# Reordered loads, conversions and squares in the opening of a gated cross-attention and FFN block

## The reference

```python
q1 = fake_quant(layernorm(x), s1, z1)            # clip(round(v / s + z), 0, 255), minus z, times s
q2 = fake_quant(ctx, s2, z2)
x  = x + tanh(g_xattn) * (q1 @ q2)
weight = U * S[None, :] @ V.T                     # U (2048, 512), V (2048, 512)
x  = x + tanh(g_ffn) * einsum('bti,oi->bto', layernorm(x), weight)
```

## Time and profile before

| what | value |
|---|---|
| median of 3 runs | 604.24 us |
| the profiled execution's own time | 604.71 us |
| its span | 602.9 us |
| TensorE matmuls busy | 582.7 us, 97% |
| VectorE busy | 381.7 us, 63% |
| ScalarE busy | 212.4 us, 35% |
| GpSimd busy | 191.4 us, 32% |
| DMA engines, opening (10 to 60 us) | 387 to 393 GB/s without a pause |

### The profile page before, as it was taken

The page is one execution under the profiler, slowest core; times in us unless marked ns, Lnnn a source line. Parts: engine busy times, 40 slices in busy tenths (PEclk is TensorE's granted clock), DMA queues, the critical chain, the costliest instruction groups (busy, mean ns, idle before and its releaser), DMA issues.

```text
span 602.9 us, 7571 instructions
## 1 busy us (share of the span) xinstructions
PE 582.7 (97%) x2816; PEld 266.4 (44%) x2816; DVE 381.7 (63%) x703; ACT 212.4 (35%) x258; POOL 191.4 (32%) x149
## 2 busy tenths in 40 slices
PE   1899999999999999999999999999999999999998
PEld 1344444444444444445444444444444444444444
DVE  6939989995288962845375975647365665735212
ACT  5798978822041432456623310303011030301000
POOL 2899650002223419726505800220404030030000
DMA  8999985639828795998835344370906345181512
GB/s 280 387 387 387 309 240 128 116 122 196 239 55 240 186 216 189 241 304 268 241 123 150 81 84 54 66 190 12 223 35 147 116 90 172 30 163 20 138 53 104
DMA packets 143828, 102.21 MB, mean 170 GB/s; under 512 B 106672, under 2 KB 106928, under 8 KB 143792
## 3 DMA queue, kind: packets, MB, share of 16 engines
q1 hardware_dynamic: 134800, 84.43, 53.1%
q10 hardware_dynamic: 8992, 17.30, 9.2%
HBM read 58.99 MB, written 16.78 MB: 126 GB/s over the span
## 4 chain that ended last, share of the span: by engine, by line
PE 75%; DMA 11%; DVE 8%; issue 3%; SPq 2%; ACT 1%; POOL 1%; DVEq 0%; ACTq 0%
PE bank L553 23%; PE bank L584 16%; PE bank L651 8%; PE bank L650 8%; PE bank L655 8%; PE bank L589 8%; DMA v_hl<-in_ctx_dram 8%; DMA xT<-xs 4%; DVE v_hl L1246 1%; DVE xn L1174 1%; DVE xs L1177 1%; DVE ring L1137 1%; SPq L311 1%; PE bank L520 1%; POOL u8r L243 1%
## 5 line engine op out<-in xcount | busy, mean ns | idle before, releaser
L553 PE MATMUL bank<-q,qT 128*128 128x512 bf16 x896 | 201.5, 380 | 0.3 <-DVE ring L1137 0.3
L553 PEld LDWEIGHTS bank<-q,qT 128*128 128x128 bf16 x896 | 87.7, 98 | 107.1 <-issue 1.5
L258 POOL TENSOR_SCALAR ring<-ring,bvec 128x2048 f32<-128x2048 f32 x16 | 32.8, 2050 | 269.7 <-DVE bvec L1119 269.7
L584 PE MATMUL bank<-v_hl,xT 128*128 128x512 f16 x512 | 115.8, 379 | 0.9 <-DMA xT<-xs 0.9
L263 POOL TENSOR_TENSOR ring<-ring,corr 128x512 f32<-128x512 f32 x64 | 87.0, 1390 | 23.2 <-ACT corr L850 22.1
L651 PE MATMUL bank<-u_hl,hbuf 128*128 128x512 f16 x240 | 91.1, 380 | 0.0
L650 PE MATMUL bank<-u_hl,hbuf 128*128 128x512 f16 x240 | 91.0, 379 | 0.0
L1137 DVE SCALAR_TENSOR_TENSOR ring<-bank,const,ring 128x512 f32<-128x512 f32 x64 | 47.6, 743 | 58.2 <-PE bank L553 55.9
L1210 DVE SCALAR_TENSOR_TENSOR ring<-bank,cy,ring 128x512 f32<-128x512 f32 x63 | 46.4, 747 | 52.8 <-PE bank L655 52.8
L252 POOL TENSOR_SCALAR q<-u8r,const 128x1024 bf16<-128x1024 uint8 x52 | 63.9, 1236 | 45.4 <-ACT u8r L756 41.7
L584 PEld LDWEIGHTS bank<-v_hl,xT 128*128 128x128 f16 x512 | 49.8, 98 | 61.2 <-DMA xT<-xs 1.9
(11 more groups left out here) (136 smaller groups left out, 493.3 us busy)
## 6 DMA issues: line engine op xcount, KB each, us to landing
out_dram<-ring SPq DMA_DIRECT2D x63, 256.0 KB, 3.5
ring<-in_x_dram SPq DMA_DIRECT2D x62, 256.0 KB, 3.9
v_hl<-in_ctx_dram SPq DMA_DIRECT2D x26, 512.0 KB, 11.5
stage<-in_ctx_dram ACTq DMA_DIRECT2D x17, 512.0 KB, 5.8
u_hl<-in_L_ffn_V_dram SPq DMA_DIRECT2D x8, 512.0 KB, 11.5
corr<-in_ctx_dram ACTq DMA_DIRECT2D x8, 512.0 KB, 6.7
stage<-in_ctx_dram SPq DMA_DIRECT2D x6, 512.0 KB, 11.5
q<-in_ctx_dram ACTq DMA_DIRECT2D x4, 512.0 KB, 8.8
```

Source lines behind the costliest of these rows:

```text
L553: mm = nc.tensor.matmul(unit_bank(t, n)[:, :], qT_of(t)[:, k, :], q2[:, n, k, :], start=(k == 0), stop=(k == KT - 1))
L584: nc.tensor.matmul(h_bank(u)[:, :], xT[:, g, half, k % 8, :], v_hl[:, k, 0, :], start=(g == 0 and a == 0 and half == 0), stop=False)
```

## The change

Four edits, all in the first 80 us:

- SyncE loads the four quarters of tile 1's x ahead of chunk 0; before, chunk 0 came first.
- The uint8 of chunks 0, 1, 3 and 4 is made by GpSimd (before: 1 to 5), and ScalarE makes those of chunks 2 and 5 (before: chunk 0). TensorE transposes tile 0 ahead of its first column sum, and takes chunks 0 and 1 one after the other.
- All eight pieces of V are loaded behind chunk 31; before, four of them stood ahead of chunks 28 to 31. ScalarE squares all of V behind the uint8 of chunk 30; before, one square stood ahead of chunk 26 and one ahead of chunk 29.
- `norm_sums(0)` stands four matmuls earlier in TensorE's list.

```diff
-        POOL_WHOLE = (1, 2, 3, 4, 5)
+        POOL_WHOLE = (0, 1, 3, 4)
...
             def op2(c):                     # GpSimd
                 b, n, i = chunk(c)
+                if c == 0:
+                    pool.wait_ge(centre_ready, 1)
                 if c in POOL_WHOLE:
...
                     pool.wait_ge(ctx_u8, act_u8(c))
-                if c == 0:
-                    pool.wait_ge(centre_ready, 1)
...
             for n in (2, 3):                # SyncE
                 load_x(0, n)
-            load_chunk(0)
             for n in range(NQ):
                 load_x(1, n)
+            load_chunk(0)
             load_chunk(1)
...
-            for c in range(12, CB - 4):
+            for c in range(12, CB):
                 load_chunk(c)
-            for i in range(4):
-                load_v(VORD[i])
-                load_chunk(CB - 4 + i)
-            for i in range(4, CQ):
+            for i in range(CQ):
                 load_v(VORD[i])
...
-            colsum(0, 0, 0, CK)             # TensorE
             q_pieces(0, 0)
             q_pieces(0, 1)
+            colsum(0, 0, 0, CK)
+            s1_part(0, 0, 0, CK)
             colsum(0, 0, CK, 2 * CK)
-            s1_part(0, 0, 0, 2 * CK)
+            s1_part(0, 0, CK, 2 * CK)
...
-            s1_part(2, NQ - 1, 0, 12)
+            s1_part(2, NQ - 1, 0, 8)
             norm_sums(0)
-            s1_part(2, NQ - 1, 12)
+            s1_part(2, NQ - 1, 8)
...
             root1(0)                        # ScalarE
-            op1(0)
             act.wait_ge(centre_ready, 1)
             op2(0)
             qT_half(0, 0)
             root1(1)
             qT_half(0, 1)
+            op1(2)
             op2(1)
+            op1(5)
             qT_half(1, 0)
...
             op1(25)
-            v_square(VORD[0])
             op1(26)
             op2(3)
             op1(28)
+            op1(29)
             column_correction(0, 2)
-            v_square(VORD[1])
-            op1(29)
             op1(30)
-            for j in VORD[2:6]:
+            for j in VORD[0:5]:
                 v_square(j)
             column_correction(0, 3)
-            for j in VORD[6:8]:
+            for j in VORD[5:8]:
                 v_square(j)
```

## The result

Over 12 executions each, the median went from 604.31 us (603.79 to 605.35) to 607.38 us (605.19 to 609.22): a ratio of 1.0044, 95% interval 1.0031 to 1.0058. The kernel became slower, by 3.07 us between the medians, and its executions lie 4.0 us apart instead of 1.6. The one that was profiled is among the quickest of them, 605.23 us with a span of 603.4 us, only 0.52 us over the profiled execution of before. So there are two questions: what the profile shows, and what the other executions lost on top.

The account below looks back on a forecast made before the run. TensorE's work plus its idle time was taken to bound the kernel. Chunk 31 2.46 us late, less 0.41 at the transpose of xs, gave +2.05; against 604.24, as the profiled execution stood 0.47 above the median, 606.3 us, range 603.2 to 607.4.

Parts of the forecast that it names:

- the turns: Last quarter: VectorE's five operations alternate with GpSimd's, a pair in 1.70 us; TensorE takes chunk 31 2.46 us late.
- Chunk 5's conversion in front of tile 1's copy: Opening: ScalarE's copy starts 2.35 us later, chunk 5's 1.55 us wait goes, and TensorE is 0.63 us late.
- wait over 2 us in one piece: Last quarter, a sign to look for: TensorE's wait for VectorE at 72.5 us is over 2 us.
- Nothing behind it gives it back: After 108 us: the +2.05 us at the transpose of xs stays to the end of the kernel.
- term of 0.41 us for the transpose of xs: At 108 us: TensorE's old wait of 0.41 us is gone, taken off the 2.46 us.
- The clock: Rival, opening: 3.2 us idle ahead of 23.81 drops TensorE to its lower clock, losing 3.2 us; 607.2 us, chance 0.10.
- matmuls 0.43 us apart after 24 us: After the opening, a sign that the forecast is wrong: TensorE's matmuls start at that spacing.
- most of a fall would vanish in chunk 31's wait: Clock rival, last quarter: of 3.2 us lost to the lower clock, 2.3 us vanish in TensorE's wait for chunk 31.
- the 0.63 us: From the opening on: tile 2's transposes, chunk 8's conversion and its q2, GpSimd and VectorE are each 0.63 us late.
- The faster rival: Opening: if chunk 5 landed by 20.4, its wait would vanish, up to 2.2 us gained in all; 602.0 us, chance 0.12.
- Squares and norm_sums(0): Behind chunk 31: squares end by 77.5, inside norm_sums(0) at 78.72 by 1.2 us; VectorE's chain is 1.60 us late.

Follow-up runs that it names:

- second experiment: The kernel after with its last quarter put back as before, so only the opening's edits are left: 606.04 us, ratio 1.0022.
- fourth: The kernel after with GpSimd's pre(0, 2) waiting until VectorE has made q2 of chunk 31: 606.76 us.
- seventh: The kernel before with the last quarter's edits alone and pre(0, 2) held back until q2 of chunk 31: 604.77 us, ratio 1.0005.
- last experiments: The last one: the kernel before with only ScalarE's order of squares changed, loads and norm_sums as they were: 605.52 us, ratio 1.0017.
- fifth experiment: The kernel after with ScalarE's conversion of chunk 5 moved behind both copies of tile 1's transposes: 604.98 us, ratio 1.0006.
- ninth experiment: The kernel after with chunk 5's conversion behind tile 1's copies, pre(0, 2) held back, chunk 31's uint8 on ScalarE, norm_sums(0) at its old place: 603.53 us, ratio 0.9991.
- first experiment: The kernel before with only the last quarter's edits (V behind all chunks, squares behind chunk 30, norm_sums(0) four matmuls earlier): 605.64 us, ratio 1.0023.
- third: The kernel after with twelve unused matmuls between tile 1's transposes and its first matmul, in place of idle time: 606.06 us.

## Why the prediction was right, and where it was not

**Direction and range:** slower, forecast 606.3 in 603.2 to 607.4; measured 607.38, at the very edge of the range. The likeliest case, the turns, was the right mechanism, but it makes up less than half of the 3.07 us. For this case alone I had forecast +2.05 us; the profiled execution, without a fall of the clock, is 0.52 us over its counterpart, and ten executions at full clock are some 1.3 us over before. That the median lies near the forecast is luck in part: a loss that I had put down as an unlikely rival came on top and filled what the turns lacked.

**Chunk 5's conversion in front of tile 1's copy** was right as a chain: copy at 22.35 (said 22.76), tile 1 at 23.40 (23.81), chunk 5's column sum at 27.30 (27.70). The 0.4 us on each is SyncE's: with the small loads first it issued chunk 5 at 9.81 instead of 10.23, and 11.37 us later it landed. What was carried on is 0.22 us, not 0.63; the cost of the opening in executions at full clock is lost in the noise (second experiment).

**The turns in the last quarter** were right one by one. Four of the five operations met GpSimd, and the last one ran freely. VectorE's five end at 66.04, 69.39 (two), 71.07 and 71.85, where I had 66.64, 68.34 and 70.04, 71.74, 72.45: each some 0.6 us early, because op2(25) began 0.42 us earlier and GpSimd began chunk 30 at 64.35, so that the first of the turns was shorter. TensorE took chunk 31 1.87 us later; the term was sized 2.46. Nor did TensorE wait over 2 us in one piece there, as I had put it: the 2.2 us are three waits, the longest of 1.30 us for chunk 27. The fourth, seventh and last experiments show by three ways that this term is caused by GpSimd's early start: held back, it costs little or nothing; started early by the squares alone, it costs the whole.

**"Nothing behind it gives it back"** was wrong. The term of 0.41 us for the transpose of xs was too small as well, for it counts from the modelled end of the matmul before. By the starts of matmuls the eight of line 589 and the wait behind them took 2.31 us before (105.81 to 108.12) and 1.73 us after, 0.58 less; 0.1 us more was made up just ahead of them. So of the 1.87 us 1.20 are left at 109.32 (108.12 before). A second such wait of before, at 268.99, is also gone in the profile after: the same matmuls start at 269.51, so 0.52 us are left, and the spans differ by 0.5. I had seen 0.9 us in two waits in the earlier trace rows and used one of them. The lines at both places, first of the kernel before and then of the kernel after at the first of them:

```profile
108.12 3.63 PE L584 MATMUL bank<-v_hl,xT 128*128 128x512 f16 x16 [0.41 <-DMA xT<-xs]
...
268.99 3.63 PE L584 MATMUL bank<-v_hl,xT 128*128 128x512 f16 x16 [0.51 <-DMA xT<-xs]
```

```profile
109.32 3.62 PE L581 MATMUL bank<-v_hl,xT 128*128 128x512 f16 x16
```

**The clock** is the step that failed: I made it a rival with a chance of 0.10, at 607.2. It is no rival but an addition, in most executions. Four sets of executions have the wait ahead of tile 1, 1.5 to 2.7 us in their profiles (the kernel after twice, the opening alone, GpSimd held back): 30 of their 48 executions report 0.997 or 0.994. In the seven sets without the wait, or with work in it, it is one of 80, and of the 91 executions of the kernel before in the three sessions none. In the two sets of the kernel after, ten executions at 0.999 or 1.000 have a median of 605.7, twelve at 0.997 one of 607.7, and the two at 0.994 took 609.2 and 609.5. So the change costs some 1.3 us at full clock, most of it by the turns (the last quarter's edits alone cost 1.1), and 2 to 4 us more in 14 of 24 executions. I had named matmuls 0.43 us apart after 24 us as a sign of being wrong. The profile after has none, but the second experiment's has just these (six from 23.35, the next at 25.89).

The Trainium skill ("TensorE: Matmul & The Clock Gate", section "Part 1: The HAM clock gate") was right that idle time brings the slow level back: here the level fell behind 2.71 us without a matmul. The rows of the second experiment put the price of that fall at 1.7 us, the part lost of 3.40 us at a granted clock of 0.51; the executions put it at some 2.

Of that rival two pieces were wrong. I said that most of a fall would vanish in chunk 31's wait. But TensorE's transposes of tile 2 stand ahead of ScalarE's conversion of chunk 8, and so everything is late together, GpSimd and VectorE as well as TensorE (second experiment). I had used that very path for the 0.63 us and left it out here.

**The faster rival** was not refused by the landing of chunk 5 alone. With the conversion behind tile 1's copies q2 of chunk 8 came only 0.3 us earlier (fifth experiment). In that profile TensorE next waits 0.80 us at 27.87 for ScalarE's quantised tile 2, and ScalarE's timeline shows why: chunk 5's conversion still stands ahead of it, so three conversions take 23.10 to 26.49 where two had taken 23.03 to 25.49 in the kernel before, and tile 2's op2 begins 1.0 us later. ScalarE has the work that GpSimd was spared. Moving it further back was not tried.

**Squares and norm_sums(0)** went as said: the last square ends at 76.9, norm_sums(0) is at 77.97 without a wait, 1.0 us later than before (said 1.6).

## What to carry to other kernels

Before taking work off an engine's list, look at what the next engine will then start earlier, and what shares a path with it there: here two squares gone from ScalarE's way cost 1 us, since GpSimd then met VectorE's tight row of operations. In a kernel that TensorE bounds, an idle stretch of it in the opening can have two prices, its length and the clock behind it; the second one comes in some executions only, so one profile can't rule it out, and the clock of every execution has to be read. And where a late engine is followed, the paths by which it delays the others have to be drawn for each cause anew.

## What the runs showed of the hardware that was not expected

In the profile of the second experiment the clock fell behind an idle stretch of TensorE of no more than 2.71 us; from 16 to 20.7 us TensorE had been busy for 3.31 us. Behind the same wait in the profiled execution of the kernel after the granted clock stayed at 1.00, although TensorE had been busy for only 2.97 us from 16 to 20.7. What decides between the two is not shown. The granted clock reads 1.00 too in the first microseconds of the trace of before, where eight transposes take 1.04 us instead of 0.61, so there the matmuls' own pace tells more than the granted clock does.

VectorE's conversions (lines 1127 and 1131) end 0.55 us behind GpSimd's operation if that was first, and with both lists full the two engines take turns of about 1.7 us. If VectorE is first, as at 52.21 in the kernel after, its conversion takes 0.73 us. VectorE's sums with a PSUM bank (line 1137) stay at 0.73 to 0.75 us beside a busy GpSimd.

Executions of one kernel with the same clock of 1.000 still lie in groups some 1.8 us apart (the ninth experiment's: 603.29 to 604.06, and 605.18 to 605.43). In the profile of the first experiment, 606.49 us, TensorE waits 1.52 us at 181 us for a transpose by DMA, and in the seventh's 1.32 us at 271 us; the other profiles have none of that kind over 0.51 us. A second cause, of 0.8 to 0.9 us, is q2 of chunk 19: 1.65 us long in the profiles of the third and the seventh (606.06 and 607.04 us), 0.73 in both profiles of the kernel after (605.23 and 605.22 us). The ten executions of that kernel at full clock lie at 605.18 to 605.27 (five), 606.11 to 606.36 (four) and 607.16, 0.9 and 1.9 us apart, which fits; but of the ones over 606 us none was profiled, so whether these two causes are all of it stays open.
